# 16-head attention: scores of a unit's two heads crossed on the two halves of the array, and the causal mask as two products on 64 rows

## The chip, the core and the metric

The program runs on one core of one Trainium2 chip. A core has five engines that run side by side and meet at semaphores: TensorE (the array of multipliers, PE in the profile, with PEld for its weight loads), VectorE (DVE), ScalarE (ACT), GpSimd (POOL), and SyncE (SP), which here only starts transfers. Products land in PSUM, eight banks of 2 KB in each of 128 partitions. The metric is the device time of one execution in microseconds; lower is better.

## What is computed

Eight layers are applied to x (16 sequences of 512 tokens, 128 channels): attention, a mixture of experts, window attention, the mixture again, a second attention, a channel mix, a gated delta rule, and the channel mix. The change is in the code of the first and the fifth layer (layers 0 and 4 in the kernel), 16 heads of 8 channels. What they compute, cut to its core (the causal mask is in layer 0 alone, rotary positions in layer 4 alone):

```
x = x + attention(layernorm(x))
q, k, v = x @ w_q, x @ w_k, x @ w_v              # 16 heads x 8 channels
scores = einsum('bhqd,bhkd->bhqk', q, k) / sqrt(8)
scores = where(causal, scores, -inf)             # layer 0
out = softmax(scores) @ v
y = out @ w_out
```

## The kernel before

Every layer is one stage behind a barrier. `attention16` is called for layer 0 with a mask and biases, for layer 4 with rotary positions. Within a call the work is a pipeline over sequences. A *step* is one call of `body`: it takes the exponentials and value products of one sequence, the row maxima of the next (`b.maxes`), and the projections of the one after (`b.project`). Steps -2 and -1 fill the pipeline, 0 to 15 are full but for their ends, 16 empties it.

A step has 32 *units*, `u` in the code. A unit serves a pair of heads, g = 0 and 1, and one tile of 128 queries or keys. The units stand in four groups of eight (*quads*, `j`); in a quad the tile index t goes 0, 0, 1, 1, 2, 2, 3, 3. Queries and keys lie in `QS` and `KS` split into bfloat16 parts: 48 rows for a head, plus a row for the shift. The head g = 0 lies in partitions 0 to 48, g = 1 in 64 to 112. So a product of a single head uses the lower or the upper half of the array's rows.

For each unit TensorE does, in this order:

- a *max product* of head 0: scores with the queries on the partitions, written to `max_bank[:, 0]`, over W = 128, 256, 384 or 512 keys as t is 0 to 3 (in layer 4 always 512). In layer 0 a *mask product* over all 128 rows follows: `ident16` times `mask_qk` adds -1e30 over the diagonal tile. VectorE then takes the maximum of each row (`reduce_max`, L660);
- the *exp products* of both heads: scores with the keys on the partitions, written to `exp_bank[:, u % 2]`, over 512, 384, 256 or 128 queries as t is 0 to 3 (in layer 4 always 512). ScalarE takes the exponential of both in one instruction (L619), and in layer 0 GpSimd clears the upper triangle (L384);
- the max product (and mask product) of head 1;
- in some units the *value products* `pv` of an earlier unit (L467): in layer 0 those of t = 0, 1, 2, 3 stand in slots 3, 5, 7 and 9 of a quad, 512, 384, 256 and 128 columns wide;
- ahead of a unit, at fixed slots (`misc_uses`), a transpose or a projection through the bank `misc`.

Each max bank has one copy for a head, so the max product of a head waits for the reduction of the unit before (`max_done`). The exp banks have two copies, so exp products wait for the exponential of two units before (`exp_done`). A value product waits for GpSimd (`masked`), and the first of a quad also for ScalarE's copy of the finished heads (`heads_kept`, L577). The order is written out by hand; engines take their instructions in that order, and there is no planner. The semaphore that the reduction waits for (`max_scores`) is raised by the mask product in layer 0 and by the max product in layer 4.

Of the kernel before, what the change touches and what calls it, by code (L numbers as in the profile page):

```python
# [15 lines left out]
MASKED = -1e30  # L16
# [118 lines left out]
PER_QUAD = SLOTS // QUADS  # L135
# [5 lines left out]
ROWS = 6 * D  # L141
# [33 lines left out]
def attention16(nc, tag, io, X, stats, identity, causal, rope, biased):  # L175
    with Stage(nc, tag) as s:
# [10 lines left out]
        if causal:  # L187
            ident16 = s.sb("ident16", [P, P], BF16)
            mask_qk = s.sb("mask_qk", [P, P], BF16)
# [5 lines left out]
        QS = s.sb("QS", [P, 2, PAIRS, T], BF16)  # L195
        KS = s.sb("KS", [P, 2, PAIRS, T], BF16)
# [10 lines left out]
        max_bank = s.ps("max_bank", [P, 2, T])  # L207
        exp_bank = s.ps("exp_bank", [P, 2, 2, T])
# [4 lines left out]
        prepared = s.sem("constants_ready")  # L213
# [11 lines left out]
        masked = s.sem("masked")  # L225
# [127 lines left out]
        def _(pool):  # L353
# [7 lines left out]
            if causal:  # L361
                nc.gpsimd.memset(mask_qk[:, :], 0.0).then_inc(split_step, 1)
                pool.wait_ge(split_step, 1)

                nc.gpsimd.affine_select(out=mask_qk[:, :], in_=mask_qk[:, :], compare_op=ALU.is_ge, fill=MASKED,
                                        base=0, pattern=[[-1, P]], channel_multiplier=1).then_inc(prepared, 1)
                nc.gpsimd.tensor_copy(ident16[:, :], identity[:, :]).then_inc(prepared, 1)
# [80 lines left out]
        def _(pe):  # L448
# [23 lines left out]
            def max_unit(b, u, g):  # L472
                to = (b.par + 1) % 2
                j, t, i = u // PER_QUAD, u % PER_QUAD // 2, 2 * (u // PER_QUAD) + u % 2
# [3 lines left out]
                last = nc.tensor.matmul(max_bank[:, g, 0:W[t]], QS[64 * g:64 * g + ROWS, to, i, t * P:(t + 1) * P],  # L478
                                        KS[64 * g:64 * g + ROWS, to, i, 0:W[t]], start=True, stop=True)
                if causal:  # L480
                    last = nc.tensor.matmul(max_bank[:, g, t * P:(t + 1) * P], ident16[:, :], mask_qk[:, :],  # L481
                                            start=False, stop=True, skip_group_check=True)
                last.then_inc(max_scores, 1)
# [6 lines left out]
            def exp_unit(b, u):  # L490
                j, kb, i = u // PER_QUAD, u % PER_QUAD // 2, 2 * (u // PER_QUAD) + u % 2
                if u % PER_QUAD == 0:
                    pe.wait_ge(shift_in[j], b.at(32, 32))
                wait_positive(pe, exp_done, b.at(SLOTS, u - 1))
                for g in range(2):
                    last = nc.tensor.matmul(exp_bank[:, u % 2, g, Q0[kb]:T],  # L496
                                            KS[64 * g:64 * g + ROWS + 1, b.par, i, kb * P:(kb + 1) * P],
                                            QS[64 * g:64 * g + ROWS + 1, b.par, i, Q0[kb]:T],
                                            start=True, stop=True)
                last.then_inc(scores, 1)  # L500

            def body(pe, b):
# [2490 lines left out]
```

## Time and profile before

| | |
|---|---|
| median of 3 runs | 6643.55 us |
| lowest, highest | 6637.37, 6680.86 us |
| the profiled execution | 6614.82 us, of which the span is 6613.1 |
| mean granted TensorE clock over the span | 0.757 |
| layer 0's attention, first max product to last output product | about 82 to 1130 us |
| layer 4's attention, likewise | about 3213 to 4167 us |

The profile is of one execution. PE rows are products, PEld rows weight loads. A granted clock of 1.00 is 2.4 GHz and 0.50 is 1.2 GHz; a value between is a mean over a stretch with both. Products are pipelined, so the end of one lies behind the start of the next, and the distance between starts tells how long the array was taken. A row of the timeline may stand for several instructions (x2, x8); it then runs from the first start to the last end.

### The profile page before, as it was taken

The page shows a single profiled execution, that of the slowest core. Times are in us where ns is not written, and L with a number is a line of the kernel's source. Part 1 is how long each engine was busy: PE and PEld are TensorE (multiplying, and loading weights), DVE is VectorE, ACT ScalarE, POOL GpSimd, SP SyncE. Part 2 cuts the span into 40 slices and gives each one's busy share as a digit, 9 for nine tenths or more (in the row PEclk, how much of TensorE's full clock was granted, in tenths as well). Part 3 has the DMA queues.
Part 4 walks back from the last instruction along what each step waited for, and adds up shares of the span by engine and source line. Part 5 has one row for each costly group of instructions (what it writes and reads, how often), then busy time and mean ns, then how long its engine had stood idle before and what let it go on. Part 6 is the DMA issues. An engine that isn't in the chain of part 4 may idle for free. (4 is left out here: it accounts for less than half of the span.)

```text
span 6613.1 us, 173017 instructions
## 1 busy us (share of the span) xinstructions
PE 4854.8 (73%) x68196; PEld 2805.3 (42%) x68198; DVE 3042.4 (46%) x6711; ACT 2274.5 (34%) x4032; POOL 1807.6 (27%) x2210
## 2 busy tenths in 40 slices
PE   5999997291899999464599999567555555777864
PEld 1333332291455555363133333344455454744433
DVE  4555544343566666433677777432111111036654
ACT  1444433051455554132266667421111110123323
POOL 2333322304555555123322221034100000013331
PEclk9797866595999999587599999778555555765557
DMA  2111110211000000111111110000100000420000
GB/s 62 38 41 41 36 35 11 79 52 38 2 2 2 2 2 2 37 51 48 41 44 41 42 45 30 2 22 29 34 18 21 12 11 9 145 71 8 6 5 27
DMA packets 218205, 205.77 MB, mean 31 GB/s; under 512 B 59347, under 2 KB 192404, under 8 KB 217622
## 3 DMA queue, kind: packets, MB, share of 16 engines
q1 hardware_dynamic: 209430, 180.20, 8.9%
q0 software_dynamic: 8192, 16.79, 0.9%
q8 instruction: 488, 8.00, 0.5%
q14 instruction: 95, 0.78, 0.0%
HBM read 131.64 MB, written 64.75 MB: 30 GB/s over the span
## 5 line engine op out<-in xcount | busy, mean ns | idle before, releaser
L660 DVE TENSOR_REDUCE l_M<-l_max_bank 128x1 f32<-128x512 f32 (+3 forms) x2048 | 1135.5, 587 | 749.2 <-PE l_max_bank L481 473.9
L619 ACT ACTIVATE l_probs<-l_exp_bank 128x1024 f32<-128x1024 f32 (+3 forms) x1024 | 880.6, 865 | 877.5 <-PE l_exp_bank L496 861.4
L478 PE MATMUL l_max_bank<-l_KS,l_QS 48*128 48x512 bf16 (+3 forms) x2048 | 748.0, 383 | 105.4 <-DVE l_M L660 53.0
L467 PE MATMUL l_out_bank<-l_probs,l_V 128*32 128x256 f32 (+2 forms) x6144 | 567.9, 452 | 27.0 <-ACT l_heads_out L577 16.9
L496 PE MATMUL l_exp_bank<-l_QS,l_KS 49*128 49x512 bf16 (+3 forms) x2048 | 471.7, 372 | 2.4 <-ACT l_probs L619 2.4
L478 PEld LDWEIGHTS l_max_bank<-l_KS,l_QS 48*128 48x128 bf16 x2048 | 182.9, 95 | 569.8 <-DVE l_M L660 371.8
L384 POOL TENSOR_SCALAR_AFFINE_SELECT l_probs<-l_probs 128x256 f32<-128x256 f32 x512 | 209.3, 409 | 703.2 <-ACT l_probs L619 697.7
L481 PE MATMUL l_max_bank<-l_mask_qk,l_ident 128*128 128x128 bf16 x1024 | 258.3, 252 | 0.0
L1778 DVE TENSOR_REDUCE l_M<-l_max_bank 128x4 f32<-128x512 f32 x256 | 175.7, 687 | 170.8 <-PE l_max_bank L1597 170.8
L2465 DVE STREAM_TRANSPOSE l_core_U<-l_core_T 128x512 f32<-128x512 f32 x64 | 45.5, 711 | 442.3 <-ACT l_core_T L2396 442.3
L843 POOL DMA_INDIRECT l_back<-main_sorted_out,l_index x128 | 122.3, 956 | 425.0 <-issue 421.8
L1438 POOL TENSOR_TENSOR l_rms<-l_rms,l_minus_half 128x20 f32<-128x20 f32 x64 | 226.2, 3534 | 11.7 <-POOL l_rms L1435 11.6
L467 PEld LDWEIGHTS l_out_bank<-l_probs,l_V 128*32 128x32 f32 x6144 | 133.5, 113 | 203.8 <-issue 120.0
L481 PEld LDWEIGHTS l_max_bank<-l_mask_qk,l_ident 128*128 128x128 bf16 x1024 | 101.6, 99 | 260.3 <-issue 234.6
L2264 PE MATMUL l_core_T_bank<-l_core_T,l_core_N 32*32 32x32 f32 x8192 | 136.6, 237 | 99.7 <-issue 97.3
L425 POOL TENSOR_TENSOR l_qk<-l_qk,l_cos 128x512 f32<-128x512 f32 x32 | 40.7, 1272 | 605.3 <-ACT l_rot L595 605.3
L1924 PE MATMUL l_in_p_bank<-l_in_taps,l_in_hT 128*128 128x384 f32 x512 | 204.6, 551 | 2.0 <-DVE l_beta L1982 2.0
L2396 ACT ACTIVATE l_core_T<-l_core_T_bank 128x512 f32<-128x512 f32 x80 | 47.8, 598 | 439.4 <-PE l_core_T_bank L2264 439.4
L941 ACT ACTIVATE l_hidden<-l_up_bank,l_own 128x128 f32<-128x128 f32 x584 | 166.9, 368 | 86.1 <-PE l_up_bank L891 86.1
L887 PE MATMUL l_t_bank<-main_identity,l_rows 128*128 128x128 f32 x148 | 49.3, 334 | 196.2 <-DMA l_rows<-main_sorted_in 196.2
L2251 POOL TENSOR_TENSOR l_core_U<-l_core_first,l_core_masks 128x512 f32<-128x512 f32 x16 | 20.2, 1263 | 619.2 <-DVE l_core_first L2462 619.2
L829 POOL DMA_INDIRECT main_sorted_in<-l_hn,l_index x128 | 124.8, 975 | 200.4 <-DVE l_hn L972 162.6
(394 smaller groups left out, 10981.5 us busy)
## 6 DMA issues: line engine op xcount, KB each, us to landing
l_parts_dram<-l_parts SPq DMA_DIRECT2D x64, 384.0 KB, 2.5
l_fir_band<-in_dr_short_dram SPq DMA_DIRECT2D x16, 1024.0 KB, 5.3
l_fir_band<-in_dr_long_dram SPq DMA_DIRECT2D x16, 1024.0 KB, 7.5
l_QS<-l_parts_dram SPq DMA_DIRECT2D x128, 96.0 KB
l_KS<-l_parts_dram SPq DMA_DIRECT2D x128, 96.0 KB
l_rows<-main_sorted_in SPq DMA_DIRECT2D x152, 64.0 KB, 1.8
main_sorted_out<-l_result SPq DMA_DIRECT2D x144, 64.0 KB, 1.5
l_QS<-l_parts_dram SPq DMA_DIRECT2D x128, 64.0 KB
```

Of the source, the lines that this page charges most:

```text
L384: nc.gpsimd.affine_select(out=diagonal, in_=diagonal, compare_op=ALU.is_ge, fill=0.0, base=0, pattern=[[0, 2], [1, P]], channel_multiplier ...
L467: last = nc.tensor.matmul(out_bank[STRIP * h:STRIP * (h + 1), q0:q1], V[:, par, kb, 4 * j + h, :], probs[:, 2 * kb + h // 2, h % 2, q0:q1] ...
L478: last = nc.tensor.matmul(max_bank[:, g, 0:W[t]], QS[64 * g:64 * g + ROWS, to, i, t * P:(t + 1) * P], KS[64 * g:64 * g + ROWS, to, i, 0:W[ ...
L481: last = nc.tensor.matmul(max_bank[:, g, t * P:(t + 1) * P], ident16[:, :], mask_qk[:, :], start=False, stop=True, skip_group_check=True)
L496: last = nc.tensor.matmul(exp_bank[:, u % 2, g, Q0[kb]:T], KS[64 * g:64 * g + ROWS + 1, b.par, i, kb * P:(kb + 1) * P], QS[64 * g:64 * g + ...
L619: nc.scalar.activation(probs[:, n, :, Q0[kb]:T], exp_bank[:, u % 2, :, Q0[kb]:T], ACT.Exp, scale=float(D) ** -0.5).then_inc(exp_done, 1)
L660: nc.vector.reduce_max(M[:, j % 2, col:col + 1], max_bank[:, g, 0:W[t]], AX.X)\
L941: last = nc.scalar.activation(hidden[:, n2, f, :], up_bank[:, n2, f * P:(f + 1) * P], ACT.Gelu, bias=own[:, n4, B1_AT + f:B1_AT + f + 1])
L1438: g.tensor_tensor(rms[:, :], rms[:, :], minus_half[:, :], ALU.pow).then_inc(rms_ready, 1)
L1778: v.reduce_max(M[:, t % 2, h:h + REP], max_bank[:, r, :].rearrange("p (a k) -> p a k", a=REP), AX.X).then_inc(max_done, 1)
L1924: nc.tensor.matmul(p_bank[:, t, 0:QKV], hT[:, n, t * P + j:t * P + j + P], taps[:, j, :], start=(j == 0), stop=(j == TAPS - 1))
L2264: last = nc.tensor.matmul(o[rows, b, :], a(rows, b), x(rows, b), start=(fresh and b == 0), stop=True, skip_group_check=True)
```

## The change

The crossing. In a unit the exp products no longer stand together as head 0, head 1. The order of the halves becomes: max product low half (head 0), exp product high half (head 1), the masks of head 0 (low), exp product low half, max product high half, the masks of head 1 (high). `max_unit` and `exp_unit` are cut into a part that waits (`max_free`, `exp_free`) and a part that multiplies. The wait for the exp bank now stands ahead of head 0's masks.

The mask. Instead of one product over all 128 rows with 128 columns, there are two over the 64 rows of the head's own half, with 64 columns each: `mask64[rows, c, :]` times `ident64[rows, :]`, c = 0 and 1. Both tables are built once by GpSimd. Layer 4 has no masks; there only the two exp products change places.

```diff
-            ident16 = s.sb("ident16", [P, P], BF16)
-            mask_qk = s.sb("mask_qk", [P, P], BF16)
+            ident64 = s.sb("ident64", [P, P // 2], BF16)
+            mask64 = s.sb("mask64", [P, 2, P], BF16)
...
-                nc.gpsimd.affine_select(out=mask_qk[:, :], in_=mask_qk[:, :], compare_op=ALU.is_ge, fill=MASKED,
-                                        base=0, pattern=[[-1, P]], channel_multiplier=1).then_inc(prepared, 1)
-                nc.gpsimd.tensor_copy(ident16[:, :], identity[:, :]).then_inc(prepared, 1)
+                for n in range(3):
+                    for c in range(2):
+
+                        base, q, row, fill = ((-64 * c, 1, -1, MASKED), (63, 0, -1, 0.0), (64 - 64 * c, 1, -1, MASKED))[n]
+                        nc.gpsimd.affine_select(out=mask64[:, c, :], in_=mask64[:, c, :], compare_op=ALU.is_ge,
+                                                fill=fill, base=base, pattern=[[q, P]],
+                                                channel_multiplier=row).then_inc(mask_step, 1)
+                    pool.wait_ge(mask_step, 2 * n + 2)
+                nc.gpsimd.tensor_tensor(ident64[:, :], identity[:, 0:64], identity[:, 64:128], ALU.add)\
+                    .then_inc(prepared, 2)
...
-                if causal:
-                    last = nc.tensor.matmul(max_bank[:, g, t * P:(t + 1) * P], ident16[:, :], mask_qk[:, :],
-                                            start=False, stop=True, skip_group_check=True)
-                last.then_inc(max_scores, 1)
+
+            def max_mask(u, g, c):
+
+                rows, at = slice(64 * g, 64 * g + 64), (u % PER_QUAD // 2) * P + 64 * c
+                return nc.tensor.matmul(max_bank[:, g, at:at + 64], mask64[rows, c, :], ident64[rows, :],
+                                        start=False, stop=True, skip_group_check=True)
...
                     if b.maxes:
-                        max_unit(b, u, 0)
+                        max_free(b, u, 0)
+                        last = max_product(b, u, 0)
+                        if not causal:
+                            last.then_inc(max_scores, 1)
                     if b.exp:
-                        exp_unit(b, u)
+                        exp_free(b, u)
+                        exp_product(b, u, 1)
+                    if b.maxes and causal:
+                        max_mask(u, 0, 0)
+                        max_mask(u, 0, 1).then_inc(max_scores, 1)
+                    if b.exp:
+                        exp_product(b, u, 0).then_inc(scores, 1)
                     if b.maxes:
-                        max_unit(b, u, 1)
+                        max_free(b, u, 1)
+                        last = max_product(b, u, 1)
+                        if causal:
+                            max_mask(u, 1, 0)
+                            last = max_mask(u, 1, 1)
+                        last.then_inc(max_scores, 1)
```

TensorE's order in layer 0, before: the second unit of a t = 2 pair, up to its value products. L478 are max products, L481 mask products, L496 exp products, L467 value products; the last figure is the number of columns.

```order
L478 MATMUL l_max_bank<-l_KS,l_QS 128x384 [waits l0_max_done]
L481 MATMUL l_max_bank<-l_mask_qk,l_ident 128x128
L496 MATMUL l_exp_bank<-l_QS,l_KS 128x256 [waits l0_exp_done]
L496 MATMUL l_exp_bank<-l_QS,l_KS 128x256
L478 MATMUL l_max_bank<-l_KS,l_QS 128x384 [waits l0_max_done]
L481 MATMUL l_max_bank<-l_mask_qk,l_ident 128x128
L467 MATMUL l_out_bank<-l_probs,l_V 32x384 [waits l0_masked]
```

The same place now (L488 max products, L494 half-masks, L509 exp products, L473 value products):

```order
L488 MATMUL l_max_bank<-l_KS,l_QS 128x384 [waits l0_max_done]
L509 MATMUL l_exp_bank<-l_QS,l_KS 128x256 [waits l0_exp_done]
L494 MATMUL l_max_bank<-l_ident,l_mask 128x64 x2
L509 MATMUL l_exp_bank<-l_QS,l_KS 128x256
L488 MATMUL l_max_bank<-l_KS,l_QS 128x384 [waits l0_max_done]
L494 MATMUL l_max_bank<-l_ident,l_mask 128x64 x2
L473 MATMUL l_out_bank<-l_probs,l_V 32x384 [waits l0_masked]
```

The first exp product and its wait have moved ahead of the first head's masks, and each mask row has become two of 64 columns. GpSimd's preparation ahead of the first projection of layer 0, before:

```order
L362 MEMSET l_mask_qk 128x128
L365 AFFINE_SELECT l_mask_qk<-l_mask_qk 128x128
L367 CAST l_ident<-main_identity 128x128
L371 COPY l_bias_v<-l_bias_col 128x128
```

and now:

```order
L362 MEMSET l_mask 128x256
L368 AFFINE_SELECT l_mask<-l_mask 128x128 x6
L372 ISA
L372 TENSOR_TENSOR l_ident<-main_identity 128x64
L377 COPY l_bias_v<-l_bias_col 128x128
```

Six selects stand where one stood; what follows on GpSimd is as before.

## Rows read from the trace of the kernel before

**Rows 1.** The page: the span, and the mask product (idle before it at the end).

```profile
span 6613.1 us, 173017 instructions
...
L481 PE MATMUL l_max_bank<-l_mask_qk,l_ident 128*128 128x128 bf16 x1024 | 258.3, 252 | 0.0
```

**Rows 2.** Busy by stretch, layer 0's steps: from:to, length, PE, PEld, DVE, ACT, POOL, clock.

```profile
183.99:263.11 79.12, 78.39 (x372) 26.59 (x368) 34.63 (x78) 26.91 (x45) 21.68 (x43) 0.55 0.10 31
...
320.62:374.79 54.17, 50.98 (x372) 21.81 (x368) 33.36 (x78) 26.58 (x45) 20.98 (x42) 1.00 0.15 45
...
sum 901.01, PE 873.26 PEld 329.32 DVE 470.27 ACT 373.61 POOL 286.87; mean PE 67.17 PEld 25.33 DVE 36.17 ACT 28.74 POOL 22.07
```

**Rows 3.** Timeline of PE at 2.4 GHz, layer 0, t = 2: start, length, line.

```profile
328.05 0.33 PE L478 MATMUL l_max_bank<-l_KS,l_QS 48*128 48x384 bf16 x1
328.31 0.23 PE L481 MATMUL l_max_bank<-l_mask_qk,l_ident 128*128 128x128 bf16 x1
328.48 0.28 PE L496 MATMUL l_exp_bank<-l_QS,l_KS 49*128 49x256 bf16 x2
328.60 0.32 PE L478 MATMUL l_max_bank<-l_KS,l_QS 48*128 48x384 bf16 x1
...
329.20 0.33 PE L478 MATMUL l_max_bank<-l_KS,l_QS 48*128 48x384 bf16 x1
...
330.17 0.85 PE L467 MATMUL l_out_bank<-l_probs,l_V 128*32 128x384 f32 x8
```

**Rows 4.** The same timeline: second quad's start and wide value product, t = 3, fourth quad.

```profile
334.99 0.23 PE L478 MATMUL l_max_bank<-l_KS,l_QS 48*128 48x128 bf16 x1
...
339.58 1.06 PE L467 MATMUL l_out_bank<-l_probs,l_V 128*32 128x512 f32 x8 [0.56 <-ACT l_heads_out L577]
...
344.27 0.39 PE L478 MATMUL l_max_bank<-l_KS,l_QS 48*128 48x512 bf16 x1
...
346.68 0.64 PE L467 MATMUL l_out_bank<-l_probs,l_V 128*32 128x256 f32 x8
...
361.77 0.23 PE L478 MATMUL l_max_bank<-l_KS,l_QS 48*128 48x128 bf16 x1
...
367.12 1.06 PE L467 MATMUL l_out_bank<-l_probs,l_V 128*32 128x512 f32 x8 [0.23 <-ACT l_heads_out L577]
```

**Rows 5.** Timeline of PE at 1.2 GHz, layer 0: t = 3, narrow units, t = 2.

```profile
505.18 0.61 PE L478 MATMUL l_max_bank<-l_KS,l_QS 48*128 48x512 bf16 x1
...
508.43 1.08 PE L467 MATMUL l_out_bank<-l_probs,l_V 128*32 128x256 f32 x8
...
645.31 0.29 PE L478 MATMUL l_max_bank<-l_KS,l_QS 48*128 48x128 bf16 x1
...
652.39 1.94 PE L467 MATMUL l_out_bank<-l_probs,l_V 128*32 128x512 f32 x8
...
654.57 0.50 PE L478 MATMUL l_max_bank<-l_KS,l_QS 48*128 48x384 bf16 x1
...
657.61 1.51 PE L467 MATMUL l_out_bank<-l_probs,l_V 128*32 128x384 f32 x8
```

**Rows 6.** Timeline of ACT, layer 0, second quad at 2.4 GHz.

```profile
335.82 1.02 ACT L619 ACTIVATE l_probs<-l_exp_bank 128x1024 f32<-128x1024 f32 x1 [2.40 <-PE l_exp_bank L496]
...
338.90 0.62 ACT L577 ACTIVATE l_heads_out<-l_out_bank 128x512 f32<-128x512 f32 x1
```

**Rows 7.** Timeline of PE at 2.4 GHz, layer 4, a unit and its value products.

```profile
3600.46 0.39 PE L478 MATMUL l_max_bank<-l_KS,l_QS 48*128 48x512 bf16 x1
3600.47 0.60 PE L496 MATMUL l_exp_bank<-l_QS,l_KS 49*128 49x512 bf16 x2
3600.70 0.38 PE L478 MATMUL l_max_bank<-l_KS,l_QS 48*128 48x512 bf16 x1
3601.00 0.64 PE L467 MATMUL l_out_bank<-l_probs,l_V 128*32 128x256 f32 x8
```

**Rows 8.** Busy by stretch (columns of rows 2): a step, and eight us within it.

```profile
374.79:437.08 62.29, 60.26 (x372) 22.66 (x369) 33.59 (x78) 26.91 (x45) 21.02 (x42) 0.81 0.12 38
...
380.00:388.00 8.00, 8.00 (x32) 1.93 (x31) 2.66 (x5) 2.72 (x6) 1.43 (x4) 0.50 0.17 60
```

More of the change, by code:

```diff
@@ L224, in attention16 @@
         heads_kept, v_cleared = s.sem("heads_kept"), s.sem("v_cleared")
-        masked = s.sem("masked")
+        masked, mask_step = s.sem("masked"), s.sem("mask_step")
         rec_ready, waited = s.sem("rec_ready"), s.sem("waited")
@@ L361, in _ @@
             if causal:
-                nc.gpsimd.memset(mask_qk[:, :], 0.0).then_inc(split_step, 1)
+                nc.gpsimd.memset(mask64[:, :, :], 0.0).then_inc(split_step, 1)
                 pool.wait_ge(split_step, 1)
-                nc.gpsimd.affine_select(out=mask_qk[:, :], in_=mask_qk[:, :], compare_op=ALU.is_ge, fill=MASKED,
-                                        base=0, pattern=[[-1, P]], channel_multiplier=1).then_inc(prepared, 1)
-                nc.gpsimd.tensor_copy(ident16[:, :], identity[:, :]).then_inc(prepared, 1)
+                for n in range(3):
[7 more added lines that the diff above has]
+                    .then_inc(prepared, 2)
             step0 = 1 if causal else 0
@@ L470, in pv, with max_free @@
                 last.then_inc(pv_done, 1)
-            def max_unit(b, u, g):
+            def max_free(b, u, g):
                 to = (b.par + 1) % 2
-                j, t, i = u // PER_QUAD, u % PER_QUAD // 2, 2 * (u // PER_QUAD) + u % 2
                 if g == 0 and u % (SLOTS // 2) == 0:
@@ L477, in max_unit, with max_product @@
                 wait_positive(pe, max_done, b.at(2 * SLOTS, 2 * SLOTS + 2 * u + g - 1))
-                last = nc.tensor.matmul(max_bank[:, g, 0:W[t]], QS[64 * g:64 * g + ROWS, to, i, t * P:(t + 1) * P],
+            def max_product(b, u, g):
+                to = (b.par + 1) % 2
+                j, t, i = u // PER_QUAD, u % PER_QUAD // 2, 2 * (u // PER_QUAD) + u % 2
+                return nc.tensor.matmul(max_bank[:, g, 0:W[t]], QS[64 * g:64 * g + ROWS, to, i, t * P:(t + 1) * P],
                                         KS[64 * g:64 * g + ROWS, to, i, 0:W[t]], start=True, stop=True)
-                if causal:
-                    last = nc.tensor.matmul(max_bank[:, g, t * P:(t + 1) * P], ident16[:, :], mask_qk[:, :],
-                                            start=False, stop=True, skip_group_check=True)
-                last.then_inc(max_scores, 1)
+            def max_mask(u, g, c):
+                rows, at = slice(64 * g, 64 * g + 64), (u % PER_QUAD // 2) * P + 64 * c
+                return nc.tensor.matmul(max_bank[:, g, at:at + 64], mask64[rows, c, :], ident64[rows, :],
+                                        start=False, stop=True, skip_group_check=True)
             def loads_before(b, to):
@@ L488, in loads_before, with exp_free, exp_product @@
                 return 16 * HALF_LOADS * n if b.i is None else b.i * (16 * HALF_LOADS) + 16 * HALF_LOADS * n
-            def exp_unit(b, u):
-                j, kb, i = u // PER_QUAD, u % PER_QUAD // 2, 2 * (u // PER_QUAD) + u % 2
+            def exp_free(b, u):
                 if u % PER_QUAD == 0:
-                    pe.wait_ge(shift_in[j], b.at(32, 32))
+                    pe.wait_ge(shift_in[u // PER_QUAD], b.at(32, 32))
                 wait_positive(pe, exp_done, b.at(SLOTS, u - 1))
[L495 to L500, printed above, removed]
+            def exp_product(b, u, g):
+                kb, i = u % PER_QUAD // 2, 2 * (u // PER_QUAD) + u % 2
+                return nc.tensor.matmul(exp_bank[:, u % 2, g, Q0[kb]:T],
+                                        KS[64 * g:64 * g + ROWS + 1, b.par, i, kb * P:(kb + 1) * P],
+                                        QS[64 * g:64 * g + ROWS + 1, b.par, i, Q0[kb]:T],
+                                        start=True, stop=True)
             def body(pe, b):
```

## The prediction

> **What bounds the kernel now.** I read the page's groups first, then busy time and granted clock sequence by sequence, then TensorE's instructions in order of time. The change touches `attention16`, which runs twice: layer 0 (causal) and layer 4 (not causal). The span is 6613.1 us; 1024 mask products of 128 rows (L481) cost 258.3 us of TensorE, all in layer 0 [rows 1].
>
> The steady part of layer 0 is 13 sequence steps and a last longer stretch that ends with the fourteenth, 901.0 us in all, 64.4 us a step. TensorE is busy 873.3 of them, VectorE 470.3, ScalarE 373.6 [rows 2]. So TensorE is the engine to look at. But a step takes 54.2 us where the granted clock is 1.00 (2.4 GHz) and 79.1 us where it is 0.55 (nearly all 1.2 GHz) [rows 2]. At 0.55 a tenth of 79.1 us, 7.9 us, ran at 2.4 GHz and did 7.9/54.2 = 15% of the step; the other 85% took 71.2 us, so a step wholly at 1.2 GHz would take about 83 us. The mean of 64.4 is then 54.2 + 0.35 x 29: about 35% of the work is done at 1.2 GHz. The clock is a second cause beside the work.
>
> Inside a unit at 2.4 GHz [rows 3]: a max product of 384 columns starts at 328.05, its mask product at 328.31. 384 columns at 2.4 GHz are 0.16 us, so 0.10 us passes in which nothing streams. The mask has 128 columns (0.05 us), and the exp products start 0.17 us behind it: 0.12 us of nothing. Exp products of 256 columns (0.11 us) are followed by the second max product after 0.12 us: no gap. So the gap appears where a product over both halves of the rows meets one over a half, four times a unit, about 0.11 us each. Both exp products lie in one row of 0.28 us: two halves stream at once.
>
> The same rows show the second limit. The next unit's max product starts at 329.20, 0.89 us behind the mask product at 328.31, though only 0.17 + 0.12 + 0.26 + 0.16 = 0.71 us of TensorE work lies between (mask to exp, exp to second max, and for that product and its mask the same 0.26 and the 0.16 of its columns as a bound). It waits for VectorE's reduction, since each half has one bank. At 2.4 GHz wide units are bound by this loop, not by TensorE. In the narrow units it is ScalarE: in the second quad the first exp starts at 335.82 and the copy of the heads at 338.90, takes 0.62 and ends at 339.52; the value product of 512 columns waits for it and starts at 339.58 [rows 4, 6].
>
> **The change, part by part.**
>
> *Layer 0, at 2.4 GHz.* Four gaps and two 128-row products go; four 64-column products on half the rows come, and the halves alternate. What this is worth is set by the two loops above.
> - Units with 384 keys (t = 2): product to first mask 0.16 instead of 0.26, plus the first half-mask's 64 columns, 0.03; from the last mask's start to the next product 0.89 less the 64 columns it no longer has, 0.86. The first unit of the pair goes from 1.15 to about 1.05. The second ends the pair: its own product, masks and one gap before the value product, 0.16 + 0.06 + 0.11 instead of 0.42. Pair and all: 2.12 [rows 3] (328.05 to 330.17) to about 1.88, -0.24.
> - t = 3: 2.41 [rows 4] (344.27 to 346.68) to about 2.23, -0.18, by the same two terms (the reduction of 512 columns is longer, the gaps are the same).
> - t = 0 and t = 1 up to the wide value product: 4.59 in the second quad, 5.35 in the fourth, where TensorE has the V projection between [rows 4]. The ScalarE chain of 3.70 us stays [rows 6]; its first exp lands about 0.15 earlier. So -0.15 where ScalarE is never idle, about -0.6 in the fourth quad, where it was; I take -0.3.
> A quad gains 0.72, a step of four quads 2.9 us: 54.2 to 51.3. Bounds: 1.5 (only the narrow-unit and t = 3 terms) and 5 us.
>
> *Layer 0, at 1.2 GHz.* Here TensorE was the bound, so more comes off. t = 2 pair 3.04 [rows 5] (654.57 to 657.61) to about 2.3: product 0.32, first mask 0.05, loop 0.89 (+0.03 at this clock), then the other half's reduction behind it and its last product. t = 3 pair 3.25 [rows 5] (505.18 to 508.43) to about 2.8. Narrow units with a transpose between, 7.08 [rows 5] (645.31 to 652.39), to about 5.5, where ScalarE's chain ends; quads without it less, I take -1.5. A quad gains 0.74 + 0.45 + 1.5 = 2.7, a step 10.8 us: 83 to 72. Bounds 7 and 14.
>
> *What moves behind a wait.* The wait for ScalarE's exp bank now stands ahead of the first half's mask products, and so ahead of VectorE's reduction of that half. In wide units ScalarE is idle much of the time (373.6 of 901.0 us busy in all, [rows 2]); in the narrow ones, where it is the bound, a late reduction costs nothing until it exceeds the slack. I price it at 0; were it not covered, a t = 0 pair would delay VectorE by up to one exp, 1.02 us [rows 6], 4 us a step.
>
> *Weights.* Each half-mask needs its own weight load, eight matrices a unit instead of six. In layer 4 a product of 512 columns (0.21 us at 2.4 GHz) is followed on the same half after 0.23 us [rows 7]: the load is hidden behind 512 columns. Behind 64 columns (0.03 us) of half the rows I have no row; the bounds for each are 0 over its own 0.03 us and the 0.11 us that a change of rows costs now [rows 3]. I take 0, since the other half streams meanwhile and the nearest row is hidden. The Trainium skill, TensorE: Matmul & The Clock Gate, Part 3 (The mechanism), says that a load overlaps running products only when the row group differs, and Part 2 prices a load of 128 columns at 128/1.2 = 107 ns. By that rule the four half-masks would cost 0.43 us a unit where the sum has 0.12, and the gain would go; [rows 7] speak against it for wide products, no row for these.
>
> *Layer 4.* No masks; only the order of the two exp products is crossed. [rows 7]: max product at 3600.46, two exp products from 3600.47 in a row of 0.60, though each lasts about 0.38, second max product at 3600.70, value product at 3601.00. The row of 0.60 means that the second exp started near 3600.69. So one exp ran beside the first max product and the other beside the second: the halves are paired already, though the program names them in another order. Value: 0, cover needed: none. Its sequences are priced at 0.
>
> *Ends.* The two steps before the steady part gain about 3 us each; six selects instead of one ahead of the first product lose 1.5 us. The last step has no masks and does not change.
>
> **Sum.** With the share of work at 1.2 GHz unchanged: 51.3 + 0.35 x (72.2 - 51.3) = 58.6 against 64.4, 5.8 x 14 = 81 us; with the ends 85. On the profiled execution (6614.8 us, span 6613.1) that gives 6530. The median of the runs is 6643.6, 29 us over that execution; the change should carry over, so I give 6560 for the median.
>
> **The clock** decides more than the work. It was never lost for want of instructions: TensorE had no idle time of note. It was 1.00 over the step that ends at 374.79 [rows 2] and 0.50 at 380 [rows 8]: it fell within the first five us of the next step, when transposes, the two narrowest units and a wait for a ScalarE copy stand together. These units now hold less streaming in nearly the same time, so this loss should come at every such step. Against that, at 1.2 GHz the steps are denser, so the clock should come back sooner. I let them cancel.
>
> **Rivals.**
> 1. The clock is mostly kept. The steps of 54.2 us show that it can be, and layer 4 with crossed halves runs in this manner. For it: denser steps. Against it: the narrow units are bound by ScalarE. With a tenth at 1.2 GHz a step takes 53.4: 11.0 x 14 + 5 = 159 us, 6485. Chance 0.15.
> 2. The clock is mostly lost: steps of 72.2 us. Then the stage loses 7.8 x 14 = 109 less 5: 6748, slower. It decides from a share of (64.4 - 51.3)/20.9 = 0.63 of the work at 1.2 GHz. For it: less streamed in the narrow units, where the clock already falls. Against: it came back in every step before. Chance 0.16, six tenths of it slower by over 1%.
> 3. The half-masks do not overlap, each costs 0.10 us or more. Then a unit at 2.4 GHz has its four gaps back under another name: no gain there, at most 4 us a step at 1.2 GHz: 0.35 x 4 x 14 = 20 us, 6624. By the skill's rule above the time would be this one. Chance 0.13.
> 4. Layer 4 gains too, because products start in the order of the program: before, first max alone, the two exps together, second max alone. Crossing would take 0.21 us from each of 512 units, 109 us, if nothing else bound them: 6450. Rows 7 speak against it. TensorE: Matmul & The Clock Gate in the Trainium skill, Part 3 (The mechanism), says that MATMULs start and end strictly in program order; by that the second max product could not have started at 3600.70 but at 3600.90. The trace differs, and decides. Chance 0.04.
> The forecast itself has 0.52.
>
> **Numbers.** The range takes the whole forecast case (share at 1.2 GHz 0.2 to 0.5, steps uncertain by 1.5 us: 6500 to 6610), rival 1 and rival 3: 6465 to 6650. A change of this kernel under 1% (66 us) can't be told from none. The forecast of 85 us is near that bound: of its 0.52, 0.36 lies beyond. With rivals 1 and 4, faster 0.55; of rival 2, 0.10 slower; the rest within.
>
> **What would show it.** Right: in a t = 2 pair at 2.4 GHz the half-mask starts 0.16 to 0.18 us behind its product and the pair takes 1.9 us; the exp product of the high half starts within 0.02 of the first max product; steps at clock 1.00 take 50 to 52 us with TensorE busy well under 90%, and VectorE's idle time in them stays. In layer 4 the pattern of [rows 7] stays, with 0.54 us from the first max product to the value product. Wrong: gaps of 0.10 ahead of each half-mask (rival 3); steps at 1.00 under 49 us (the loops were misread); steps whose mean no longer fits a share near 35% at 1.2 GHz; layer 4 changed by more than 10 us.

## The result, and the profile after

| | before | changed |
|---|---|---|
| median of 16 runs, same chip | 6663.38 us | 6613.81 us |
| lowest, highest | 6615.55, 6706.79 | 6587.06, 6647.24 |
| span of the profiled execution | 6613.1 us | 6585.3 us |
| mean granted clock over that span | 0.757 | 0.747 |

The ratio is 0.9941, 95% interval 0.9919 to 0.9963: 39 us of 6663 (25 to 54), where 85 were forecast. A ratio in this document is not the quotient of two medians (here 0.9926, 49.6 us) and leaves out executions more than 1.5% above the fastest of the same kernel: four of the twelve of `e1_cross_only`, two of `e3_split_128`, one of `e6_before_unrolled`. The time lies in the range and on the forecast side, but the gain is about half of the forecast, and within the 1% that was said to be hard to tell from nothing. Only layer 0 differs by more than the stages scatter from run to run: 1081.1 us before, 1043.3 after, from first to last product.

The page after: the half-masks are 2048 rows of 0.22 us where 1024 rows of 0.25 us stood [rows 1], and max products now wait for VectorE (204.5 us).

```profile
span 6585.3 us, 175076 instructions
...
L488 PE MATMUL l_max_bank<-l_KS,l_QS 48*128 48x512 bf16 (+3 forms) x2048 | 713.3, 392 | 204.5 <-DVE l_M L686 153.2
...
L494 PE MATMUL l_max_bank<-l_ident,l_mask 64*128 64x64 bf16 x2048 | 252.3, 219 | 0.0
```

Inside a unit it went as forecast. The timeline of TensorE at 2.4 GHz, a t = 2 pair (columns of rows 3):

```profile
699.24 0.33 PE L488 MATMUL l_max_bank<-l_KS,l_QS 48*128 48x384 bf16 x1
699.24 0.28 PE L509 MATMUL l_exp_bank<-l_QS,l_KS 49*128 49x256 bf16 x1
699.36 0.32 PE L488 MATMUL l_max_bank<-l_KS,l_QS 48*128 48x384 bf16 x1
699.41 0.22 PE L494 MATMUL l_max_bank<-l_ident,l_mask 64*128 64x64 bf16 x2
...
701.07 0.85 PE L473 MATMUL l_out_bank<-l_probs,l_V 128*32 128x384 f32 x8
```

The high half's exp product starts with the low half's max product (699.24), the first half-mask 0.17 us behind its product (0.26 before, [rows 3]). The pair takes 1.83 us (2.12 before, 1.88 forecast); a t = 3 pair 2.20 (701.86 to 704.06; 2.41 before, 2.23 forecast). No gap stands ahead of the half-masks. The loads of their weights are hidden: the row x2 at 699.41 runs 0.22 us from the first start to the last end, and one half-mask in it lasts 0.19, so the second starts 0.03 us behind the first, and 0.03 is what its 64 columns take.

At 1.2 GHz it is the same. A t = 2 pair there takes 2.26 us (3.04 before [rows 5], 2.3 forecast):

```profile
769.21 0.50 PE L488 MATMUL l_max_bank<-l_KS,l_QS 48*128 48x384 bf16 x1
...
771.47 1.51 PE L473 MATMUL l_out_bank<-l_probs,l_V 128*32 128x384 f32 x8
```

The t = 3 pair behind it takes 2.74 us (773.95 to 776.69; 3.25 before, 2.8 forecast).

The steps tell where the gain went. Busy time by stretch (columns of rows 2): two steps of layer 0, then thirteen from 126.56; below them, of the kernel before, the same thirteen.

```profile
692.23:745.58 53.35, 39.39 (x437) 21.42 (x433) 32.27 (x79) 26.53 (x45) 22.03 (x42) 1.00 0.15 48
745.58:814.64 69.06, 60.16 (x432) 29.70 (x432) 31.86 (x77) 26.58 (x45) 20.08 (x41) 0.58 0.10 34
126.56:943.89 817.33, 681.61 (x5594) 341.18 (x5592) 411.83 (x999) 344.98 (x583) 270.21 (x533) 0.70 0.12 39
```

```profile
128.90:941.48 812.58, 783.59 (x4762) 300.86 (x4762) 436.28 (x1000) 346.82 (x583) 271.58 (x532) 0.81 0.12 38
```

TensorE is busy for 102 us less in these thirteen steps, and they take 5 us more. The granted clock fell from 0.81 to 0.70. The step at 1.00 takes 53.35 us, and 2.73 of those are new: TensorE stands idle ahead of the transposes that open the next step.

```profile
745.58 0.95 PE L526 MATMUL l_misc<-main_identity,l_hn 128*128 128x128 f32 x4 [2.73 <-issue]
```

"Issue" means that no semaphore was late. Such idle time stands at each of the five jumps of the loop that holds two steps (3.11, 3.09, 3.01, 2.73, 1.97 us: 13.9 in all); before there was none over 1 us in layer 0. Without it the step at 1.00 is 50.6 us, where 51.3 was forecast. What the profile of this one execution gains lies in the end of the stage behind the thirteen steps: 189.7 us at a clock of 0.63 before (941.48 to 1131.20), 151.4 at 0.83 after.

So two things are to be explained: the idle time at the jumps, and the clock.

### The profile page after: what moved, and what is told of

It reads as the page before. It is cut to its first block and busy times, and to the rows that moved or that the text cites. A ratio compares the mean times of both kernels' runs of the same rounds, so it can differ in the third digit from the quotient of the medians.

```text
span 6585.3 us, 175076 instructions
## 1 busy us (share of the span) xinstructions
PE 4691.4 (71%) x69220; PEld 2849.9 (43%) x69222; DVE 3010.0 (46%) x6711; ACT 2271.3 (34%) x4032; POOL 1804.5 (27%) x2215
## 5 line engine op out<-in xcount | busy, mean ns | idle before, releaser
L686 DVE TENSOR_REDUCE l_M<-l_max_bank 128x1 f32<-128x512 f32 (+3 forms) x2048 | 1103.1, 585 | 746.9 <-PE l_max_bank L494 490.3
L488 PE MATMUL l_max_bank<-l_KS,l_QS 48*128 48x512 bf16 (+3 forms) x2048 | 713.3, 392 | 204.5 <-DVE l_M L686 153.2
L473 PE MATMUL l_out_bank<-l_probs,l_V 128*32 128x256 f32 (+2 forms) x6144 | 585.4, 463 | 40.9 <-ACT l_heads_out L603 27.6
L509 PE MATMUL l_exp_bank<-l_QS,l_KS 49*128 49x512 bf16 (+3 forms) x2048 | 583.8, 378 | 6.0 <-ACT l_probs L645 5.9
L488 PEld LDWEIGHTS l_max_bank<-l_KS,l_QS 48*128 48x128 bf16 x2048 | 167.6, 96 | 681.6 <-DVE l_M L686 504.4
L494 PE MATMUL l_max_bank<-l_ident,l_mask 64*128 64x64 bf16 x2048 | 252.3, 219 | 0.0
L494 PEld LDWEIGHTS l_max_bank<-l_ident,l_mask 64*128 64x128 bf16 x2048 | 210.8, 115 | 61.7 <-issue 28.2
L473 PEld LDWEIGHTS l_out_bank<-l_probs,l_V 128*32 128x32 f32 x6144 | 135.6, 114 | 216.2 <-issue 122.2
L1950 PE MATMUL l_in_p_bank<-l_in_taps,l_in_hT 128*128 128x384 f32 x512 | 204.5, 551 | 2.0 <-DVE l_beta L2008 2.0
```

Of the source, the lines that this page charges most:

```text
L473: last = nc.tensor.matmul(out_bank[STRIP * h:STRIP * (h + 1), q0:q1], V[:, par, kb, 4 * j + h, :], probs[:, 2 * kb + h // 2, h % 2, q0:q1] ...
L488: return nc.tensor.matmul(max_bank[:, g, 0:W[t]], QS[64 * g:64 * g + ROWS, to, i, t * P:(t + 1) * P], KS[64 * g:64 * g + ROWS, to, i, 0:W[ ...
L494: return nc.tensor.matmul(max_bank[:, g, at:at + 64], mask64[rows, c, :], ident64[rows, :], start=False, stop=True, skip_group_check=True)
L509: return nc.tensor.matmul(exp_bank[:, u % 2, g, Q0[kb]:T], KS[64 * g:64 * g + ROWS + 1, b.par, i, kb * P:(kb + 1) * P], QS[64 * g:64 * g + ...
L686: nc.vector.reduce_max(M[:, j % 2, col:col + 1], max_bank[:, g, 0:W[t]], AX.X)\
L1950: nc.tensor.matmul(p_bank[:, t, 0:QKV], hT[:, n, t * P + j:t * P + j + P], taps[:, j, :], start=(j == 0), stop=(j == TAPS - 1))
```

## The experiments

Each session ran its own runs of the kernel before. A ratio below is to those, with its 95% interval. The changed kernel itself ran only in the session of the result, so its 0.9941 is compared with the ratios of others across sessions.

**First session: the parts of the change, and the loop** (before: 6604.92 us, 27 runs). The theory: TensorE's loop of two steps has grown from 1739 to 1995 instructions, no longer stays in the engine, and must be fetched again at each jump. The rivals stand in the expectations.

`e1_cross_only`: the changed order, with the mask product of before (`ident16` times `mask_qk`, 128 rows); head 1's alike.

```diff
-                        max_mask(u, 0, 0)
-                        max_mask(u, 0, 1).then_inc(max_scores, 1)
+                        max_mask(u, 0).then_inc(max_scores, 1)
```

> The crossed order alone, with the mask product of before (128 rows, 128 columns). TensorE's loop over two steps has as few instructions as before the change. If the gain comes from the half-masks and crossing is worth nothing, as it was in layer 4 (842.8 us for fifteen steps' distance after, 843.1 before): 0.99 to 1.01 of before, steps at clock 1.00 of 54 us. If crossing is worth something by itself (the product of the low half no longer stands alone in a unit): one gap and up to 0.1 us a unit less, 52 us a step. By the theory that the loop's length causes the new idle time ahead of HT: none of these gaps here (each under 0.5 us) and no fetches of instructions (q8) between 440 and 560 us.

Measured: 6590.88 us, 0.992 (0.9881 to 0.996), with executions from 6499 to 6652; the quotient of the medians is 0.9979, so no gain is shown. Its steps at clock 1.00 take 54.7 us, half a microsecond longer than before; what the executions differ by goes with the clock, whose mean over the span runs from 0.753 to 0.780 in them. The order alone takes no work off the path. No idle time at the jumps.

`e2_half_masks_only`: the order of before, with half-masks.

```diff
                     if b.maxes:
                         max_free(b, u, 0)
                         last = max_product(b, u, 0)
-                        if not causal:
-                            last.then_inc(max_scores, 1)
+                        if causal:
+                            max_mask(u, 0, 0)
+                            last = max_mask(u, 0, 1)
+                        last.then_inc(max_scores, 1)
                     if b.exp:
                         exp_free(b, u)
-                        exp_product(b, u, 1)
-                    if b.maxes and causal:
-                        max_mask(u, 0, 0)
-                        max_mask(u, 0, 1).then_inc(max_scores, 1)
-                    if b.exp:
-                        exp_product(b, u, 0).then_inc(scores, 1)
+                        exp_product(b, u, 0)
+                        exp_product(b, u, 1).then_inc(scores, 1)
```

> The half-masks alone, in the order of before (head 0's product and masks, both exp products, head 1's product and masks). The loop has the instructions of the changed kernel. If crossing is needed: each half stands alone beside its own masks and the unit is longer than in the changed kernel, 52.5 us or more for a step at clock 1.00 without its gap (50.6 in the changed kernel). If the array pairs the halves anyway, as in layer 4: 50.6 again and a time within 0.3% of the changed kernel. By the loop's length: the gaps of 2 to 3 us ahead of HT at the five jumps are here too.

Measured: 6564.95 us, 0.9932 (0.9905 to 0.9959), the same as the changed kernel's 0.9941. A step at 1.00 without a jump takes 50.5 us:

```profile
250.45:300.94 50.49, 39.75 (x437) 21.69 (x433) 32.14 (x79) 26.54 (x45) 20.88 (x42) 1.00 0.16 49
```

The whole of the gain is the half-masks'. TensorE pairs the halves by itself when no product over all rows stands between them. The timeline of this kernel, a t = 2 pair at 2.4 GHz, shows how:

```profile
257.48 0.33 PE L488 MATMUL l_max_bank<-l_KS,l_QS 48*128 48x384 bf16 x1
257.62 0.33 PE L488 MATMUL l_max_bank<-l_KS,l_QS 48*128 48x384 bf16 x1
257.66 0.22 PE L494 MATMUL l_max_bank<-l_ident,l_mask 64*128 64x64 bf16 x2
```

In the program head 0's half-masks and both exp products stand between the two max products. The second max product, on the high half, starts at 257.62, ahead of the half-masks of the low half at 257.66 (0.18 us behind their own product), which stand before it in the program. The pair takes 1.84 us (to its value products at 259.32), against 1.83 in the crossed order.

`e3_split_128`: before, each mask product cut in two of 64 columns. Same work, longer loop.

```diff
-                    last = nc.tensor.matmul(max_bank[:, g, t * P:(t + 1) * P], ident16[:, :], mask_qk[:, :],
-                                            start=False, stop=True, skip_group_check=True)
+                    for c in range(2):
+                        last = nc.tensor.matmul(max_bank[:, g, t * P + 64 * c:t * P + 64 * c + 64], ident16[:, :],
+                                                mask_qk[:, 64 * c:64 * c + 64],
+                                                start=False, stop=True, skip_group_check=True)
```

> The kernel before with each mask product cut into two of 64 columns over the same 128 rows: the same work and order, but as many instructions in TensorE's loop as in the changed kernel. Theory of the loop's length: fetches of instructions (q8) in every step, gaps of 2 to 3 us ahead of HT at the five jumps (13 us), and the clock falls in some of them (up to 11 us each): 1.002 to 1.008 of before. Rival, that the gaps come from the crossed order or the moved wait: no gap over 1 us, no q8 between 440 and 560 us, a time within 0.2% of before.

Measured: 6640.83 us, 1.0047 (1.0021 to 1.0073). Idle times of 3.05, 2.83, 2.66, 2.72 and 2.70 us at the five jumps, with no semaphore late, ahead of the transposes as in the changed kernel. Neither the crossing nor the moved wait is in this kernel: the number of instructions makes the idle time. The transfers show it. The DMA view of the changed kernel over two steps of layer 0, 445 to 568 us (transfers, MB, share):

```profile
q8 instruction: 10, 0.16, 0.6%
```

These are ten blocks of 16 KB. In the same view of before q8 has six transfers from 263 to 371 us, in the first turn of the loop, and none from 371 to 1011 us. From 437 to 560 us `e3_split_128` fetches eight, `e1_cross_only` none.

`e4_unrolled_l0`: the changed kernel, TensorE's loop of layer 0 written out (a flag, left out below, keeps the loop of the other engines and of layer 4).

```diff
-            with eng.Fori(0, len(LOOPED) // 2) as i:
-                body(eng, Part(i, LOOPED.start))
-                body(eng, Part(i, LOOPED.start + 1))
+            for n in LOOPED:
+                body(eng, Part(None, n))
```

> The changed kernel with TensorE's loop of layer 0 written out, so that there is no jump. Theory of the loop's length: the five gaps go (12.9 us in the profile of the changed kernel), and the clock no longer falls in them, which it did at four of the five jumps for 27 to 34 us at 1.2 GHz each, 9 to 11 us a time: 13 us if the clock falls anyway in the narrow units that follow, up to 55 us if it does not. 0.992 to 0.998 of the changed kernel. Rival, that less streaming in the narrow units alone loses the clock: 13 us or less, and a mean granted clock of layer 0 that stays at 0.72.

Measured: 6556.61 us, 0.993 (0.9903 to 0.9956), 8 us under `e2_half_masks_only`, less than the two intervals can tell. The idle times are gone, steps at 1.00 take 50.8 us, but most steps still lose the clock (0.64 to 0.82). The expected 13 to 55 us did not come in the timed runs: against this pair the jumps cost their idle time at most, and the clock falls without them too.

**Second session: the clock, and layer 4** (before: 6609.72 us, 23 runs).

`e5_unrolled_both`: as `e4_unrolled_l0`, and the loop of layer 4 written out too.

> The changed kernel with TensorE's loop written out in both attention layers. Layer 4's loop has as many instructions as layer 0's in the changed kernel (592 and 716 products as written, 848 and 967 instructions in all, but more of them split in two) and had an idle time of 2.8 us ahead of HT every two steps before the change as well. If that is the jump: five times 2.8, 14 us less than with layer 0 alone written out, all in layer 4: 980 us for it instead of 994.8; 0.991 of before. If it is the wait for the layernorm or another engine: layer 4 stays at 995.

Measured: 6565.52 us, 0.9918 (0.9889 to 0.9947). Layer 4 takes 1003.4 us instead of 994 to 995: the expectation failed. TensorE's idle time there moved to the next wait, and ScalarE shows why (timeline of PE, then of ACT, at a jump in layer 4):

```profile
3396.23 0.38 PE L543 MATMUL l_misc<-main_identity,l_M 128*16 128x128 f32 x1 [3.60 <-ACT l_hT L614]
```

```profile
3394.66 1.02 ACT L649 ACTIVATE l_probs<-l_exp_bank 128x1024 f32<-128x1024 f32 x1 [5.60 <-issue]
```

ScalarE stands 5.60 us with no semaphore late, and only then, at 3395.58, comes to the copy (L614) that TensorE waits for. It does so five times in layer 4, 27.8 us in all: as often as its own loop jumps. So the longer stall seems to have covered the shorter while both engines jumped together; no run has ScalarE's loop written out.

`e6_before_unrolled`: the same on the kernel before.

> The kernel before with TensorE's loop written out in both layers. Layer 0 had no idle time over 1 us at its jumps and fetched nothing there, so by the loop's length nothing is gained in it; layer 4 gains 14 us: 0.998 of before, the mean granted clock unchanged. Rival: written out, layer 0 must fetch all the time, which costs something by itself (steps at clock 1.00 over 54.5 us).

Measured: 6579.97 us, 0.995 (0.9915 to 0.9985), steps at 1.00 of 54.5 us instead of 54.2, layer 4 at 1002.2 us. So the steps grew by 0.3 us and layer 4 by 8, where 14 fewer were expected; what was gained is the clock's, whose mean over these executions was 0.766 against 0.757. The expectation had it unchanged. The granted clock is itself a record with gaps: a step of 77.41 us (128.52 to 205.93) reads 1.00 here, though its length is that of a step at 1.2 GHz. A step's length is the safer sign.

`e7_filled`: `e5_unrolled_both` with repeated max products in the narrow units of layer 0 (the *filling*). Nothing is left out.

```diff
-                        last = max_product(b, u, 0)
+                        for _ in range((5, 3, 1, 1)[u % PER_QUAD // 2] if causal and b.exp else 1):
+                            last = max_product(b, u, 0)
```

> As e5, and in the narrow units of layer 0 head 0's max product is repeated, five times over for t = 0 and three times for t = 1 (same result, nothing left out), so that TensorE streams while it would wait for ScalarE's exp bank. Theory that the clock falls because the narrow units stream less than before: the share of layer 0's work at 1.2 GHz drops from 0.4 to under 0.2, its mean clock rises over 0.85, and the time falls by 50 us or more against e5 although there is more to do. Rival, that the clock's falls have nothing to do with these units: clock as in e5, and 16 units with 512 more columns, at most 0.2 us each at 2.4 GHz, 0 to 3 us a step, 0 to 45 us more than e5.

Measured: 6520.64 us, 0.9851 (0.9809 to 0.9893): 45 us less than `e5_unrolled_both` by more work (50 or more were expected). A step at 1.00 costs 1.7 us more (52.5 against 50.8), but from 302.73 us on the clock holds at 0.94 to 1.00 in every step:

```profile
410.75:463.23 52.48, 41.90 (x485) 21.93 (x481) 32.02 (x79) 26.56 (x45) 20.86 (x42) 1.00 0.15 47
```

`e8_one_mask`: the changed kernel with less work, the first of the two half-masks of each head left out.

```diff
-                        max_mask(u, 0, 0)
                         max_mask(u, 0, 1).then_inc(max_scores, 1)
...
-                            max_mask(u, 1, 0)
                             last = max_mask(u, 1, 1)
```

> The changed kernel, looped, with one of the two half-masks of a head left out: the diagonal tile's first 64 keys aren't masked in the maxima. The loop has 128 products fewer, as many as before the change. By the loop's length: no idle time over 1 us ahead of HT, no q8 between 440 and 560 us, 13 us less than the changed kernel by that alone. A half-mask's own price at 2.4 GHz: 0.03 us of columns each, hidden for one head beside the other's exp product: step 50.6 to 49.5 at most. Were each 0.10 us (load not hidden): 44 or so.

Measured: 6667.7 us, 1.0087 (1.0059 to 1.0115): slower than the changed kernel, and than before, where 13 us less than the changed kernel were expected. No idle time at the jumps and no fetches, as the loop's length says. But the clock falls at the same places in every step from 384.73 on, and comes back for a few microseconds only:

```profile
453.02:521.30 68.28, 58.80 (x372) 24.78 (x369) 31.73 (x78) 26.59 (x45) 20.93 (x42) 0.58 0.12 35
```

With the filled kernel this is the plainest evidence: a half-mask taken off each head, clock 0.58; max products added, clock 0.94 to 1.00. What a half-mask costs a step at 2.4 GHz can't be read here, since no step ran wholly at that clock. The Trainium skill, TensorE: Matmul & The Clock Gate, Part 1 (The HAM clock gate), says that the throttled state is the default and activity releases it; these two traces agree (68.3 us with less to do, 52.5 with more).

**Third session: the change at a nearly equal clock, and a better kernel** (before: 6627.37 us, 16 runs).

`e9_filled_l0` is `e4_unrolled_l0` with the filling of `e7_filled`; `e10_filled_less` the same with

```diff
-                        for _ in range((5, 3, 1, 1)[u % PER_QUAD // 2] if causal and b.exp else 1):
+                        for _ in range((3, 2, 1, 1)[u % PER_QUAD // 2] if causal and b.exp else 1):
```

`e11_before_filled` is the kernel before, looped, with the filling of `e7_filled` on its head 0, `e12_after_filled_looped` the changed kernel, looped, with the same.

> The changed kernel, layer 0's TensorE loop written out (layer 4's not), head 0's max product of layer 0 five times over for t = 0, three times for t = 1. Writing out layer 4's loop cost 8.6 us in the profile (1003.4 against 994.8), so this should stand 8 us below e7: 0.984 of before, layer 0 in 951 us, a mean clock of 0.77. If layer 4's 8.6 us were chance: as e7.

> As e9, but three times over for t = 0 and twice for t = 1. Each repeat costs time at 2.4 GHz (steps of 52.5 us with the full filling, 50.8 without). If half of it keeps the clock as well: steps of 51.6, layer 0 some 10 us shorter than e9. If the clock falls again: between e4 (0.993) and e9.

> The kernel before, looped, with the same filling of the narrow units. Its steps at 2.4 GHz are 54.2 us, some 55.5 with the filling. If the clock holds, layer 0 loses its stretches at 1.2 GHz: 0.990 of before, and the distance of e9 to it is what the change is worth at an equal clock, 3 to 4 us a step, 50 us. If filling does not help here: 1.000 to 1.003. The loop has 1931 instructions by this, between the 1739 that stayed in the engine and the 1995 that did not: either is possible at its jumps.

> The changed kernel, looped, with the same filling. Against e9 it has the five jumps: 13 us by their length alone, and if an idle time of 2 to 3 us costs the clock by itself, as seen at four of five jumps of the changed kernel, up to 11 us more for each: 13 to 65 us over e9, 0.986 to 0.994 of before.

| | median | ratio, interval | layer 0 in the profile |
|---|---|---|---|
| `e9_filled_l0` | 6505.20 us | 0.9802 (0.9764 to 0.984) | 957.2 us |
| `e10_filled_less` | 6555.18 | 0.9855 (0.9808 to 0.9901) | 1015.7 |
| `e11_before_filled` | 6597.15 | 0.9951 (0.9924 to 0.9979) | 1069.3 |
| `e12_after_filled_looped` | 6512.00 | 0.9815 (0.9775 to 0.9854) | 962.4 |

The pair that matters is the last two: same filling, both with idle times at all five jumps (14 us each), and the same mean clock over their whole executions (0.771 both). Their medians lie 85.2 us apart (0.9871), and their intervals don't meet. Two steps that show it, each with a jump's idle time (`e11_before_filled`, then `e12_after_filled_looped`):

```profile
457.58:516.58 59.00, 54.59 (x420) 23.60 (x417) 34.03 (x78) 26.77 (x45) 22.19 (x43) 0.99 0.14 44
```

```profile
396.25:451.26 55.01, 41.98 (x485) 22.55 (x481) 32.70 (x79) 26.56 (x45) 22.04 (x42) 0.99 0.15 47
```

Both rows hold one idle time (2.87 and 2.83 us) at their end; the difference is 4.0 us a step at 2.4 GHz, 56 over fourteen. The rest should come off where the clock is at 1.2 GHz. Part of it may be the clock's: within layer 0 it was not quite equal, 0.870 and 0.902 in the two profiled executions. By the lengths of their steps some 0.22 and 0.18 of the work ran at 1.2 GHz; with one share for both, the fourteen steps would differ by some 79 to 85 us, an estimate. `e11_before_filled` did not reach its expected 0.990, since the filling held the clock less well there.

Filling half as much did not hold the clock in the profiled execution, the slowest of six (6507 to 6573 us): from 361.85 us on, every step of `e10_filled_less` took 61.4 us at a clock of 0.75, so the expected 51.6 did not come. One of them:

```profile
361.85:423.24 61.39, 51.75 (x461) 25.51 (x457) 32.06 (x79) 26.58 (x45) 20.95 (x42) 0.75 0.12 40
```

`e11_before_filled` also settles the loop's length from the other side: 1931 instructions are already too many. `e12_after_filled_looped` cost 7 us over `e9_filled_l0`, not 13 to 65. That is so although the clock falls at the jumps: in the profiles of the four looped kernels with these idle times (the changed one, `e3_split_128`, `e11_before_filled`, `e12_after_filled_looped`) the granted clock goes to 0.50 within 3 us of 19 of the 20 jumps, and was there already at the twentieth. `e9_filled_l0` beats both kernels, by 2% of before; all but 7 us of that is had with the two lines of filling alone on the changed kernel.

## Why the prediction was wrong

**The work: right.** Pairs of t = 2 and t = 3 came within 0.06 us of the forecast at either clock, and the step at 2.4 GHz at 50.6 us for 51.3: the narrow units gained more than the 0.3 us a quad that was taken (0.43, 0.21, 0.42 and 0.63 us in the four quads from 692.23 us on). At 1.2 GHz a step is near the 72 of the sum: the step of 69.06 us at 0.58 ran 16% of its time, 11 us, at 2.4 GHz, which is 11/50.6 = 22% of its work; the other 78% took 58 us, 74 for a whole one. At a nearly equal clock the change is worth 85 us in the timed runs, and 79 to 85 by the estimate above. That this is the sum's own figure is in part luck: the pair is filled and has the jumps, and the sum had another share of work at 1.2 GHz.

That the half-masks' weights cost nothing (0.03 us from one to the next, the time of their columns), and that layer 4 gains nothing (842.8 us from the first step's transposes to the fifteenth's, 843.1 before), held too. The rule of the Trainium skill, TensorE: Matmul & The Clock Gate, Part 3 (The mechanism), that a load overlaps running products only in another row group, did not hold here: the two half-masks of a head stand on the same rows with different weights, 0.03 us apart, and the pair got shorter by 0.29 us. One reading was loose without an effect on the sum: the 901.0 us of rows 2 are twelve steps and a stretch of two, which makes the fourteen that it divides by.

**What failed first: "I let them cancel".** The sum kept the share of work at 1.2 GHz at 35%. By the rows above it rose. The thirteen steps take (817.3 - 13.9)/13 = 61.8 us without the jumps, so the share is (61.8 - 50.6)/(74 - 50.6) = 0.48; by the same sum before it was (62.5 - 54.2)/29 = 0.29. The prediction had named the mechanism in rival 2, less streamed in the narrow units, and gave it 0.16: it asked for 0.63 to turn the sign. Its range did allow a share of up to 0.5, but the time it gave kept the 35%, as if a rise were no likelier than a fall. The two effects that it set against each other were not equal. What it wrote against the loss, that denser steps bring the clock back sooner, has no support: the one kernel with still less to do (`e8_one_mask`) sat at 0.58. In the thirteen steps of the two profiles, at these prices, the work took off some 68 us, the jumps added 14 and the higher share 59: the 5 us more that were seen.

New falls also come some 17 us into a step, in its second quad (granted clock 1.00 from 568.45, then 0.50 from 585.40). In the thirteen steps of before the clock fell some 4 to 5 us into a step; its only later falls, at 208.46 and 631.71 us, came 24 us into a step whose clock had already fallen and had been back for 3.4 us.

```profile
568.45:585.40 16.95, 13.04 (x148) 6.86 (x145) 9.47 (x24) 9.82 (x16) 7.26 (x14) 1.00 0.19 48
585.40:612.60 27.20, 24.25 (x163) 11.88 (x159) 12.09 (x31) 9.45 (x18) 9.50 (x18) 0.50 0.18 59
```

**What was missed: the loop.** "Four 64-column products come" was costed by columns and loads, never by the length of the loop that holds them. Layer 4's steps, with 436 products each, showed an idle time of nearly 3 us every two steps in the profile of before, while layer 0's with 372 showed none; the changed layer 0 has 436. It costs 13.9 us of idle time in the profile, and 7 to 8 in the timed runs by two pairs of kernels whose intervals overlap; in both pairs the kernel without jumps also has its loop written out, which makes a step 0.2 to 0.4 us longer.

**The sum put right.** 85 us of work, less 7 to 14 at the jumps, less what the clock took: 39 were measured, so some 32 to 39 (21 to 28 by the medians' 49.6). This last figure is a remainder. No kernel changed the clock's share alone by this much, and single profiles scatter: the one of before ended its stage at 0.63, the one after at 0.83. What decides whether the clock falls at a given step, so that executions of one and the same kernel lie up to 150 us apart (`e1_cross_only`), stays open.

## What to carry to other kernels

Where a stretch already hovers between 1.2 and 2.4 GHz, a change that makes TensorE do less there must be priced at both clocks and with the share moved towards 1.2 GHz; then see whether harmless repeated products in the waits hold the clock. Here they took the changed kernel from 0.9941 to 0.9815 of before, and the kernel before to 0.9951. Count the instructions of a loop as well as their time: here a loop that just stayed in its engine could be lengthened only at the price of a stall at each jump. And compare two versions at the same granted clock before judging their work.

## What the runs showed of the hardware

- TensorE ran loops of 1739 instructions (products, weight loads, and the loop's own; one turn has 1723 records in the trace, and 1915 and 1980 for the longer ones) without fetching any from the second turn on, and fetched those of 1931 and 1995 all the time, in blocks of 16 KB, with 2.0 to 3.1 us of idle time at the jump back. The Trainium skill, Runtime: NRT & Kernel Launch, "Instruction fetch mechanics", tells of 16 KiB blocks, 2048 instructions for TensorE and a stall when a jump's target isn't there. The stall and the blocks agree; that 1931 already stall lies below its figure.
- Written out, a step took 0.2 to 0.4 us more at 2.4 GHz than in a loop that stays in the engine (54.5 against 54.2 before), and layer 4 got slower by 8 to 9 us, with ScalarE standing 5.60 us at what looks like its own jump.
- TensorE lets a product on one half of the rows pass another that waits on the other half: with half-masks the order written by hand made no difference (50.5 us a step in the old order, 50.6 in the crossed one, and a max product that starts at 257.62 ahead of half-masks at 257.66 that precede it in the program). With the mask product over all rows the crossed order took 54.7 us, the old one 54.2.
- Two products of 64 columns on the same 64 rows, each with its own weights, started 0.03 us apart at 2.4 GHz: the load between them cost nothing.
- Less work made the program slower: 1.0087 of before with one half-mask a head, 0.9941 with two, 0.9802 with two and up to four further copies of a max product (and layer 0's loop written out).
